# FFN of a fused cross-attention and mixture-of-experts kernel: the one-hots of four batches turned at once, and the output bias as four products of 32 array rows

## The reference, cut to what matters

```python
logits = xt @ Wg.T                      # xt: layer-normed tokens, Wg: 8 x 256
top1 = argmax(logits)
xhat = (xt - mean(xt)) * rsqrt(var(xt) + 1e-5)
for e in range(8):
    h = gelu((xhat * s_e + b_e) @ w1_e + bb1_e)      # 64 hidden values
    y += (top1 == e) * (h @ w2_e + bb2_e)            # bb2: 8 x 256, the output bias
```

## Time and profile before

| | before |
|---|---|
| median of three runs | 1419.14 us |
| profiled execution | 1419.81 us |
| its span | 1418.0 us |
| mean granted clock of TensorE | 0.994 of full speed |
| PE, PEld busy | 1385.2 us (98%), 1200.7 us (85%) |
| DVE, ACT, POOL busy | 1160.4 us (82%), 986.7 us (70%), 486.0 us (34%) |

### The profile page before, as it was taken

The page is one execution under the profiler, slowest core; times in us unless marked ns, Lnnn a source line. Parts: engine busy times, 40 slices in busy tenths (PEclk is TensorE's granted clock), DMA queues, the critical chain, the costliest instruction groups (busy, mean ns, idle before and its releaser), DMA issues.

```text
span 1418.0 us, 40277 instructions
## 1 busy us (share of the span) xinstructions
PE 1385.2 (98%) x15394; PEld 1200.7 (85%) x15394; DVE 1160.4 (82%) x2757; ACT 986.7 (70%) x1668; POOL 486.0 (34%) x667
## 2 busy tenths in 40 slices
PE   7899999999999999999999999989999999999998
PEld 6788888888888888888888888877888888888887
DVE  4788888888888888888888888876887887888775
ACT  4577777777777777777777777756766666676663
POOL 4223332233223332233223332324544544444430
PEclk9999999999999999999999999999999999999999
DMA  5657765667557765666566765643343444434322
GB/s 161 171 150 184 180 172 150 185 167 180 143 156 180 179 160 151 178 170 179 152 161 177 181 159 147 161 118 104 98 129 106 120 112 114 124 103 133 106 76 75
DMA packets 173671, 207.47 MB, mean 146 GB/s; under 512 B 20087, under 2 KB 125866, under 8 KB 173482
## 3 DMA queue, kind: packets, MB, share of 16 engines
q1 hardware_dynamic: 173482, 204.89, 54.5%
HBM read 69.26 MB, written 33.81 MB: 73 GB/s over the span
## 4 chain that ended last, share of the span: by engine, by line
PE 89%; DVE 5%; ACT 2%; issue 2%; DMA 1%; SPq 0%; POOL 0%; ACTq 0%; DVEq 0%; POOLq 0%
PE s_ps L1382 13%; PE pp_ps L1253 11%; PE pv_ps L1201 8%; PE st_ps L1184 8%; PE s_ps L1156 8%; PE pp_ps L1226 7%; PE st_ps L1407 7%; PE pp_ps L1261 6%; PE pp_ps L1407 6%; PE pv_ps L1209 4%; PE pp_ps L1247 3%; DVE negmax L860 2%; PE pp_ps L1346 2%; PE t_ps L1175 2%; PE t_ps L1357 1%
## 5 line engine op out<-in xcount | busy, mean ns | idle before, releaser
L667 ACT ACTIVATE pT<-st_ps 128x1024 f32<-128x1024 f32 x256 | 262.9, 1027 | 102.7 <-PE st_ps L1184 101.5
L860 DVE TENSOR_REDUCE negmax<-s_ps 128x8 f32<-128x1024 f32 x256 | 311.3, 1216 | 21.3 <-PE s_ps L1156 21.2
L517 POOL TENSOR_TENSOR q_parts<-q,q_parts 128x1024 bf16<-128x1024 f32 x31 | 66.4, 2140 | 395.3 <-ACT q_parts L661 395.3
L725 ACT ACTIVATE pT<-s_ps,c 128x512 f32<-128x512 f32 x128 | 87.8, 689 | 115.9 <-PE s_ps L1382 112.7
L1156 PE MATMUL s_ps<-k_packed,q_packed 96*128 96x128 bf16 x2048 | 158.3, 220 | 7.0 <-DVE negmax L860 4.9
L1382 PE MATMUL s_ps<-k_packed,w_hi 128*128 128x512 f32 x512 | 165.0, 413 | 0.0
L1184 PE MATMUL st_ps<-q_packed,k_packed 98*128 98x128 bf16 x2048 | 158.6, 221 | 0.0
L1156 PEld LDWEIGHTS s_ps<-k_packed,q_packed 96*128 96x128 bf16 x2048 | 128.3, 98 | 25.6 <-DVE negmax L860 16.5
L1184 PEld LDWEIGHTS st_ps<-q_packed,k_packed 98*128 98x128 bf16 x2048 | 121.0, 98 | 25.5 <-issue 25.5
L535 POOL TENSOR_TENSOR xb<-xin,bo_all 128x256 f32<-128x256 f32 x128 | 90.4, 727 | 146.4 <-DMA x_scratch<-xb 131.4
L1201 PE MATMUL pv_ps<-pT,v 128*32 128x128 f32 x4096 | 138.5, 276 | 0.0
(11 more groups left out here) (203 smaller groups left out, 3699.1 us busy)
## 6 DMA issues: line engine op xcount, KB each, us to landing
q_packed<-q_parts SPq DMA_DIRECT2D x186, 256.0 KB, 4.2
k_packed<-k_parts SPq DMA_DIRECT2D x186, 256.0 KB, 4.5
xin<-in_x_dram SPq DMA_DIRECT2D x32, 512.0 KB, 4.0
cin<-in_ctx_dram SPq DMA_DIRECT2D x32, 512.0 KB, 4.5
out_dram<-xb SPq DMA_DIRECT2D x32, 512.0 KB, 3.2
x_scratch<-xb SPq DMA_DIRECT2D x32, 256.0 KB, 4.8
x_scratch<-xb SPq DMA_DIRECT2D x64, 128.0 KB, 4.6
k_parts<-mask_scratch SPq DMA_DIRECT2D x32, 256.0 KB, 4.1
```

The source lines that it names most:

```text
L667: a.activation(pT[u % 2][:], st_ps[:], ACT.Exp, scale=DH ** -0.5).then_inc(s_exp, 1)
L725: a.activation(hidden32[m], h_ps[m % 2], ACT.Gelu, bias=c1[:, m:m + 1]).then_inc(f_he, 1)
L860: v.tensor_reduce(own, s_ps[:].rearrange("p (h s) -> p h s", s=P), AX_X, ALU.max, negate=True).then_inc(s_red, 1)
```

## The change

The one-hots of the four batches of a group stand in one tile, `onehot_by_batch`: per token 4 batches x 32, of which 24 hold the one-hot three times, eight columns apart. One transpose turns all of it, so that rows 32b to 32b + 31 of `onehotT` belong to batch b. ACT's copy is 128 x 128 instead of 96 x 512. The bias is laid out likewise: `b2_strips` holds, for each batch's 32 rows, the 24 rows of the three parts. The four bias products leave `outputs`' last pass and stand together behind it (`output_bias`), each with the 32 rows of the array that its batch's strip stands on, into the same four banks as before, each raising `f_y`. Group 0 keeps the old form, in a room borrowed from `b2f`. The mask's store to DRAM takes 128 partitions of 128 tokens. To fill the strips, DVE clears their tile in group 12 and SP issues four small loads each at the start of groups 14, 15 and 16; one more tile is cleared at the start.

```diff
-        onehotT = [sb(f"onehotT{n}", [3 * EP, GT], BF16) for n in range(2)]
+        onehot_by_batch = sb("onehot_by_batch", [P, GB, EP // E, E], BF16)
+        onehotT = [sb(f"onehotT{n}", [P, P], BF16) for n in range(2)]
+        onehotT_first = b2f[:].bitcast(BF16)
...
-                sp.dma_start(rows_n, onehotT[n % 2][0:E, :]).then_inc(f_md, 16)
+                sp.dma_start(rows_n.rearrange("k (b t) -> b k t", b=GB), onehotT[n % 2][:]).then_inc(f_md, 16)
...
+            def load_strips(k):
+                sp.wait_ge(s_b2c, 1)
+                for b in range(GB):
+                    sp.dma_start(b2_strips[b * EP + k * E:b * EP + (k + 1) * E, :],
+                                 b2p[k * EP:k * EP + E, :]).then_inc(s_strip, 16)
+
             def group(g):
+                if g in (14, 15, 16):
+                    load_strips(g - 14)
...
-                a.copy(onehotT[n % 2][:], onehotT_ps(n)).then_inc(f_oh, 1)
+                a.copy(onehotT[n % 2][:] if n else onehotT_first, onehotT_ps(n)).then_inc(f_oh, 1)
...
+                elif at_step == (12, 3):
+                    dve.wait_ge(s_ffw, FFW)
+                    v.memset(b2_room[:], 0.0).then_inc(s_b2c, 1)
...
-                v.tensor_tensor(onehot[:, :, :, 0:E], first[:].unsqueeze(2).broadcast_to([P, GB, 3, E]),
+                v.tensor_tensor(onehot_by_batch[:, :, 0:3, :] if n else onehot[:, :, :, 0:E], first[:].unsqueeze(2).broadcast_to([P, GB, 3, E]),
...
-                for b in range(GB):
-                    mm = t.transpose(onehotT_ps(n)[:, b * T:(b + 1) * T], onehot[:, b, :, :], ident_bf[:])
+                if n == 0:
+                    for b in range(GB):
+                        mm = t.transpose(onehotT_ps(0)[:, b * T:(b + 1) * T], onehot[:, b, :, :], ident_bf[:])
+                else:
+                    mm = t.transpose(onehotT_ps(n), onehot_by_batch[:].rearrange("p b k e -> p (b k e)"), ident_bf[:])
...
-                if m == MC - 1:
-                    t.matmul(o, onehotT[n % 2][:, tok], b2p[:], start=False, stop=True).then_inc(f_y, 1)
+                if m == MC - 1 and n == 0:
+                    t.matmul(o, onehotT_first[:, tok], b2p[:], start=False, stop=True).then_inc(f_y, 1)
+
+            def output_bias(n):
+                pe.wait_ge(s_strip, STRIPS)
+                for b in range(GB):
+                    strip = slice(b * EP, (b + 1) * EP)
+                    t.matmul(o_ps(n, b), onehotT[n % 2][strip, :], b2_strips[strip, :], start=False,
+                             stop=True).then_inc(f_y, 1)
...
                 for m in range(MC):
                     outputs(n, range(GB), m)
+                output_bias(n)
```

More of the change, by code:

```diff
@@ L43, in xattn_moe @@
     EC = P // HID
-    assert T == P and D == 256 and GROUPS % 2 == 0 and GROUPS > 12 and GROUPS * GB == BATCH
+    assert T == P and D == 256 and GROUPS % 2 == 0 and GROUPS > 18 and GROUPS * GB == BATCH
     Q_PARTS = (0, 0, 0, 1, 1, 2)
@@ L62, in xattn_moe @@
     x2_v = x2_dram.rearrange("(g b) t d -> g t b d", b=GB)
-    mask_dram = [nc.dram_tensor(f"mask_scratch{n}", [E, GT], BF16, kind="Internal").ap() for n in range(2)]
+    mask_dram = [nc.dram_tensor(f"mask_scratch{n}", [EP, GT], BF16, kind="Internal").ap() for n in range(2)]
     with ExitStack() as stack:
@@ L94, in xattn_moe @@
         b2f = sb("b2f", [3 * EP, D])
-        b2r = sb("b2r", [3 * EP, D])
+        b2_room = sb("b2_room", [P, D])
+        b2r = b2_room[0:3 * EP, :]
         b2p = sb("b2p", [3 * EP, D], BF16)
         rank = sb("rank", [P, E])
+        b2_strips = b2_room[:].bitcast(BF16)[:, 0:D]
         xin = [sb(f"xin{n}", [P, GB, D]) for n in range(2)]
@@ L191, in xattn_moe @@
             "bias_rows_transposed", "bias_columns_kept", "expert_rows_transposed", "expert_columns_kept"))
+        s_b2c, s_strip = sem("b2_strips_cleared"), sem("b2_strips_loaded")
         s_c1T, s_c1, s_boT, s_ffw = (sem(n) for n in (
@@ L219, in xattn_moe @@
         FFW = 17
+        STRIPS = 16 * 3 * GB
         FFW_FREE = (0, 3, 6, 8)
@@ L282, in onehotT_ps @@
         def onehotT_ps(n):
-            return (pv_ps[0:3 * EP, 0:GT // 2] if n else pp_ps[0][0:3 * EP, GT // 2:GT]).bitcast(BF16)
+            return (pv_ps[:, 0:P // 2] if n else pp_ps[0][0:3 * EP, GT // 2:GT]).bitcast(BF16)
         def ffn_load(sp, n):
@@ L307, in load_mask @@
                 for e in range(EC):
-                    of_half = rows_n.rearrange("(m e) t -> e m t", e=EC)[e]
+                    of_half = rows_n[0:E, :].rearrange("(m e) t -> e m t", e=EC)[e]
                     sp.dma_start(mask_rows[n % 2][e * HID:(e + 1) * HID, :, :],
@@ L336, in ffn_stats_of @@
                 count = at(GB, n, b + 1)
-                dve.wait_ge(s_b2z, 2)
+                dve.wait_ge(s_b2z, 3)
                 dve.wait_ge(f_bn, count)
@@ L939, in ffn_weights @@
                     dve.wait_ge(s_ffw, FFW - 4)
-                    v.tensor_tensor(b2r[:], b2f[:], b2p[:], ALU.subtract).then_inc(s_ffw, 1)
+                    v.tensor_tensor(b2r, b2f[:], b2p[:], ALU.subtract).then_inc(s_ffw, 1)
                 elif at_step in ((10, 3), (10, 6)):
@@ L1009, in _ @@
             v.memset(onehot[:].rearrange("p b k e -> p (b k e)"), 0.0).then_inc(s_b2z, 1)
+            v.memset(onehot_by_batch[:].rearrange("p b k e -> p (b k e)"), 0.0).then_inc(s_b2z, 1)
             for b in range(GB):
```

## The result

The changed kernel takes 1428.34 us (median of 4 runs, 1427.8 to 1429.21), the kernel before 1419.47 on the same chip (4 runs, 1418.7 to 1420.74): a ratio of 1.0059 with an interval of 1.0046 to 1.0071. It is slower, as forecast, but by 8.9 us where the forecast had 4.0, and it lies outside the range that ended at 1427.0. The profiled execution took 1428.09 with a span of 1426.2, so 8.2 us are there to be found.

A forecast was written before the change was run, and what follows sets the result against it. PE was taken to bound the FFN. Turns -5.3, bias -2.3, stall +10.8 and end +0.75 sum to +4.0 us, giving a median of about 1423.1; 8-in-10 range 1417.5 to 1427.0, the forecast's own 1420 to 1426.

The forecast's parts named there:

- Entering the array's division: PE, switching to 32-row products behind the last w2 product: 0.10 us to enter, 0.10 + 0.11 to leave.
- rival C: The four strip products run one after another on PE, 0.107 us apart: 1424.1 us; chance 0.13.
- the drain: PE's idle pause at a change of the array's division, before strip weights load: charged at 0.10 us.
- rival B: Row strips need no drain on PE, so additions start 0.10 us earlier: about 1419.6 us; chance 0.10.
- The turn: PE turns the one-hots with one product instead of four: 0.17 us less, 31 times, -5.3 us.
- The stall: PE waits for DVE's late copy of the logits behind bunched additions: 0.40 us in 27 groups, +10.8 us.
- a term that the prediction had put at nothing: ACT's copy of the turned one-hots shrinks from 512 to 128 columns, said to cost nothing or little.
- The term of the end: The last group's additions on DVE end later after the last product: +0.75 us.
- Rival A: DVE catches up using its idle time, no stall, PE keeps the gain: about 1412.3 us; chance 0.12.
- Rival D: A second wait, from the mask's late store or `onehot`: 0.2 us more in 27 groups, 1428.5 us; chance 0.07.
- the one on the loads: Twelve bias-strip loads at the head of SP in groups 14 to 16: taken as 0, bounds 0 to 4.

The follow-up runs named there:

- kernel 1: Changed kernel with the twelve strip loads issued later on SP, behind the load of x: 1422.53 us, ratio 1.0015 to the kernel before.
- kernel 7: Changed kernel with the twelve strip loads spread, one at the head of each of groups 14 to 25: 1423.38 us, ratio 1.0024 to the kernel before.
- kernel 6: kernel 1 with each strip product right behind its own batch's last output product: 1446.8 us, ratio 1.0201 to the kernel before.
- kernel 3: kernel 1 with DVE's copy of the logits placed ahead of the masking of the first hidden block: 1410.93 us, ratio 0.9937 to the kernel before.
- kernel 4: kernel 1 with the four strip products opening the sums, so each batch's last w2 product closes its own: 1409.82 us, ratio 0.9927 to the kernel before.
- kernel 5: Kernel before with only its four 96-row bias products moved together behind the last output product, no strips: 1425.18 us, ratio 1.0038.
- kernel 2: Kernel before plus the twelve loads at the head of groups 14 to 16, into a tile nothing reads: 1425.29 us, ratio 1.0036.
- kernel 8: Changed kernel with the second load of the maxima in groups 14 to 16 issued ahead of the first packing: 1436.17 us, ratio 1.0114 to the kernel before.

## Why the prediction was right in its direction and wrong in its size

The direction doesn't hang on the loads: kernels 1 and 7, in which these cost next to nothing, are slower than the kernel before too (1.0015 and 1.0024).

**The steps that held.** Entering the array's division was put at 0.10 and leaving it at 0.10 and 0.11: the strips' weights came at 0.21 and `hidden` at 0.54, forecast 0.21 and 0.56. The four products started at one time, so rival C is out. The Trainium skill, TensorE: Matmul & The Clock Gate, Part 3 (Packing small matmuls), with its 4 ns between products of different row groups, is in line with this: the trace has the four within 0.01 us in every group. The pause that the prediction calls the drain exists for row strips too, so rival B is out, and kernel 6 shows it three more times a group. The turn spares 0.15 (from its start to the first output product 0.04 in place of 0.19; forecast 0.17):
```profile
1223.64 0.23 PE L1390 MATMUL pv_ps<-ident_bf,onehot_by_batch 128*128 128x128 bf16 x1
1223.68 0.36 PE L1428 MATMUL st_ps<-w_hi,q_packed 128*128 128x256 f32 x1
```

**The stall.** The view of waits and kernels 3, 4 and 5 show it: bunching alone brings it (5), moving the copy past the masking removes it with the bunching in place (3), and closing the sums one by one removes it with the strips in place (4). The Trainium skill's rule that tiling doesn't speed up the emptying of PSUM (TensorEngine Tiling (Array Packing), PSUM Bottleneck) agrees as far as it goes: a queued addition takes 0.33 us with the strips, and in kernel 5 without them. But it isn't the tiling that makes the emptying a bottleneck here: kernel 5 has the loss without it, and kernel 4 has the tiling without the loss.

The stall's size was 0.36 and not 0.40: from the last product of w2 at 0, the first addition came at 0.53 (0.555), the statistics at 1.87 (1.915), masking at 3.47 (3.525) and the copy at 4.07 (4.155). Every link is some hundredths early. Of the 28 equal periods 25 are 13.91 or 13.92 (forecast 13.97), one without statistics is 13.55, and two, of groups 8 and 24, are 14.27; in these DVE has an extra idle 0.27 ahead of the masking that the profile puts down to no one. The mask's way through DRAM is not what makes it. From the issue of its store to that of its reload now lie 2.1 us in place of 1.37, and it lands 1.8 to 2.5 us behind the first product of its group; masking begins at 3.03, and in groups 8 and 24 the mask had landed at 2.24 and 1.85. What makes these two is open.

In all the FFN cost 2.5 us for the 4.0 forecast. The missing 1.5 divide like this. The 28 periods cost 3.4 for 3.9. Group 0 gained 0.48 for 0.17: its last turns of xhat wait for ACT, whose copy of the one-hots takes 0.27 in place of 0.58, a term that the prediction had put at nothing. And the program ends 0.6 sooner behind the last addition (3.4 us in place of 4.0), in all seven profiled kernels with the strips and in none of the three without; no run says why. The term of the end itself held: counted from the last group's first product the last addition comes 0.71 later, forecast 0.75.

Rival A did not come, since DVE could not catch up; what was said against it (the idle time lies before the products) is seen in the 1.92 of idle time. Rival D, a second wait in the FFN, had the time 1428.5, next to the 1428.34 measured; that is chance, since the mask landed in time and no wait of PE for `onehot` came.

**The step that failed** is the one on the loads: "The twelve small loads of the bias strips stand at the head of SP in groups 14 to 16. Three like them took 3.0 at the start; SP idles in the attention phase and I take 0, with 0 to 4 as bounds." They cost 5.2 us, more than the upper bound of 4. Kernel 2 has them alone (+5.25 in the three groups), kernels 1 and 7 take them out of the way (+0.15 and -0.46). That SP was idle over the phase was true and beside the point: the queue is served in order, and its idle time at this place was 1.5 us in front of the packing for an issue of 2.70. Issued 1.3 us later, its transfers were still keeping the DMA engines busy when a small load was issued on which PE waits. That load landed 5.2 us behind its issue in place of 2.0; 2.0 of the delay were covered and 1.2 became idle time of PE. SP's timeline in group 14 of the kernel before (above) shows the 1.5 us, and the prediction doesn't use it; the text itself named "anything that moves the 960 us before the FFN by more than a microsecond" as what would make it wrong. With 5.2 in that place and the FFN as forecast the sum would have been +9.2 for the +8.2 of the trace, and the median 1428.3. That this meets the measured 1428.34 is in part luck, since the FFN's part was 1.5 too high.

**What stays open.** That the maxima land late because the DMA engines are still busy with the packing rests on the traces: landed 5.1 to 5.5 us behind the issue at a busy share of 1.07 or 1.08 (changed kernel and kernel 2), 2.3 to 3.0 at 0.58 to 0.74 (kernel 7), 1.9 to 2.1 at 0.35 to 0.42 (groups 14 to 16 of the kernel before and of kernel 1), and 1.9 at 0.21 to 0.25 where the load goes out ahead of the packing (kernel 8). No experiment moved that share alone. The 1.6 us of the three groups that are not PE's wait for the maxima have no cause shown. The 1.11 us by which group 14 begins later are small against what the traces differ by there (438.2 to 443.9 us in the nine others).

## What to carry to other kernels

Price each DMA issue that is put at the head of an in-order queue against the idle time of that queue at that very place, and look what it pushes: an engine's idle share over a phase says nothing here, and spreading the same loads over twelve groups left none of their cost in the three (86.19 us for 86.65) and at most 0.5 us in the twelve. Where small products close several sums at once, the engine that empties the banks gets all its work at one time and whatever stands behind it in its queue is late; open the sums with the small products instead (kernel 4: 0.9927 of the time before, with the same instructions that give 1.0015 at the end in kernel 1). A switch between whole-array and strip products cost some 0.3 us in and out here (0.10, then 0.10 and 0.11); four products at once gained 0.09 of 0.63, and single ones lost 0.29 each (kernel 6).

## What was not expected of the hardware

Issuing four loads of 8 rows of 512 bytes on SP took 2.70 us, 0.68 each, while a transfer of 512 KB took 0.44 to issue (`cin`): here the issue's time does not follow the bytes. In kernel 8 the clock fell behind PE's longest idle (2.10 us, a stretch at full clock before it). The view by stretches (PE, PEld, DVE, ACT, POOL, then granted clock, DMA share, GB/s):
```profile
460.00:467.00 7.00, 5.19 (x80) 4.61 (x78) 5.07 (x11) 5.38 (x11) 1.16 (x1) 1.00 1.06 241
467.30:470.50 3.20, 3.20 (x19) 2.91 (x19) 0.42 (x1) 1.29 (x2) 1.41 (x2) 0.50 0.71 182
```
From 467.30 PE is busy all the time and is granted 0.50, the 1.2 GHz level; so this stall cost more than its own 2.1 us. Groups 15 and 16 have two more such stretches, 501.40 to 508.00 and 535.50 to 542.20 us, behind idle times of 1.91 and 1.84. PE is busy for 13.9 us in the three; at full clock the same work would take about half (an estimate from these numbers), so the clock is some 7 us of what kernel 8 lost (12.8 in the three groups and 2.1 in group 17). Behind the 1.19 us of idle time in the changed kernel the granted clock stays at 1.00 (464.20 to 467.50). The length of an idle time alone doesn't decide it: an idle 1.30 us stands ahead of the half-clock stretch of the last attention group in kernel 1 and at the same place in kernel 3, where the clock stays at 1.00.
